# Two batches' factor products in a row, with smaller edits around them, in a two-layer LoRA kernel

## The chip, the cores and the metric

The kernel runs on one core of one Trainium2 chip. The metric is the device time of one execution in microseconds (us); three runs of the kernel before gave 287.18, 287.47 and 287.54.

## The reference

Two residual layers follow each other, each a linear layer with a bias and with a low-rank adapter that each of the 8 batches picks by an index (x is 8 x 256 x 1024, rank 16, 32 adapters each, all float32):

```python
def layer0(x, idx, W, b, As, Bs):
    h = einsum('bti,bir->btr', x, As[idx])
    return einsum('bti,oi->bto', x, W) + b + 2 * einsum('btr,bro->bto', h, Bs[idx])
def layer1(x, idx, W, b, A, B):
    h = einsum('bsd,brd->bsr', x, A[idx])
    return einsum('bsd,od->bso', x, W) + b + einsum('bsr,bor->bso', h, B[idx])
x = x + layer0(x, itok_B_0_23, ...)
x = x + layer1(x, itok_B_6_15, ...)
```

## The kernel before

**The algebra.** The kernel multiplies the two weight matrices once, (I + W0^T)(I + W1^T), and then applies the one product to all batches. Both levels use a Strassen-like scheme on 2 x 2 quadrants of 512 x 512: seven products M1 to M7 for the weights, and for each batch seven products p1 to p7 of 128 x 512 by 512 x 512, from four quadrants A11, A21, A12, A22 of x, four sums S1 to S4 of them, and seven right sides (B11, B21, B22, T1 to T4). Each float32 operand is split into a high part (a cast to fp32r, on ScalarE, ACT in the profile) and a low part (a subtraction, on VectorE, DVE), and a product takes three fp32r passes: high by high, high by low, low by high. A product p is so twelve matmuls of 512 columns (`product`, L1194).

**What is added by small products.** The adapters and biases come in through a stack of 98 rows per batch. The kernel builds, ahead of the batches, `g` (`gt_passes`, `turn`, `g_copy`), the rows `r` (`r_passes`, with `s_t` times `b1_raw` in plain float32 at L1155 and L1160) and the bias rows `c` (`ones_b` times `bias_sum`, L1173, in plain float32, one bank for each half). The rows r, the rows b1 and the rows c, each as high and low parts, go out to `rb_rows` in DRAM (`bounce`, L319, and L327) and come back for each batch (`load_rb`). For each batch, `h_product` (L1217) multiplies x by the batch's two factor matrices: 8 matmuls of 256 columns in plain float32, whose left sides have 32 columns each, on four column tiles of the array. For batch 0 the sum runs over the high and the low parts of x, so there are 16. `stack_h` on DVE adds the four partial results and splits them; `ranks` (L1207) puts stack times rows on top of a bank.

**Order.** Each engine has one hand-written order. TensorE (PE): M1, M2, g's first half, M7, `turn(0)`, M3, s_t's product, r's passes, M6, c, g's second half, M5, M4 (with `turn(1)` inside), then the batches. Batch 0 goes p1, p6, h(0), p7, p2, p5, p4, `fill_z` (a rank product that waits for u4), h(1), p3; a later batch b goes p1, p6, p2, p5, p7, h(b+1), p4, fill_z, p3. In M1 the last step over k goes through all four banks with the high pass and then through all four with the low ones; M2 adds onto these banks once ACT has copied each one out (`m1_kept`). There is one buffer `xr` for the raw x of a batch (in the place of v22), and x of batch b+1 is loaded quadrant by quadrant over x of batch b as its users finish (`load_x`, L263). SyncE (SP) issues nearly all DMAs in one order.

Of the kernel before, what the change touches and what calls it, by code (L numbers as in the profile page):

```python
# [39 lines left out]
def lora_pair(nc, xT, U11, V11, W0, W1T, A0, B0T, A1T, B1, b0, b1, idx0, idx1, out):  # L40
# [22 lines left out]
    with ExitStack() as ctx:  # L63
# [11 lines left out]
        raw_a = sb("raw_a", [P, 4, QUAD], F32)  # L75
# [11 lines left out]
        aa = sb("aa", [P, 2 * HALF], F32)[:, 0:HALF].rearrange("p (s k c) -> p s k c", s=2, k=KT)  # L87
# [5 lines left out]
        s_t = sb("s_t", [P, BR], F32)  # L93
# [17 lines left out]
        b1_hl = b0w_flat[:, 0:2 * D].rearrange("p (s n) -> p s n", s=2)  # L111
# [4 lines left out]
        c_hl = [c_rows[32 * part:32 * part + B, :] for part in range(2)]  # L116
# [25 lines left out]
        xr = raw("v22").rearrange("p (j n) -> p j n", j=4)  # L142

        x_first = [late[:, part, :].rearrange("p (j n) -> p j n", j=4) for part in range(2)]
# [5 lines left out]
        stage_q = raw_a[:, 0:3, :].rearrange("p s (k n) -> p (s k) n", n=HALF)  # L150
# [4 lines left out]
        u4 = [stage_q[:, 2, :], stage_q[:, 8, :]]  # L155
        c21, c22, c12 = u2, u3, u4

        def s_raw(j, b):

            if b == 0 and j in (S3, S4):  # L160
                return xr[:, A21 if j == S3 else A12, :]
            return {S1: rows[:, 0, :], S2: rows[:, 1, :], S3: stage_q[:, 9, :], S4: stage_q[:, 10, :]}[j]

        def x_raw(j, b):
            return xr[:, j, :] if j <= A22 else s_raw(j, b)
# [15 lines left out]
        x_landed = [sem(f"x_landed{j}") for j in range(4)]  # L181
        a0_landed = [sem(f"a0_landed{s}") for s in range(2)]
        r_bounced = sem("r_bounced")
        bounced = sem("bounced")
# [40 lines left out]
        st_step = sem("st_step")  # L225
        r_summed = sem("r_summed")
# [3 lines left out]
        b1_hi_made = sem("b1_hi_made")  # L230
        b1_lo_made = sem("b1_lo_made")
        c_hi_made = sem("c_hi_made")
        c_lo_made = sem("c_lo_made")
# [29 lines left out]
        def _(sp):  # L263
            def load_x(b):
                for j in (A11, A21, A12, A22):
                    if b >= 1:

                        if j != A21 or b == 1:
                            sp.wait_ge(op_lo[j], b)
                        for s in {A11: (S2, S3), A21: (S1, S3), A12: (S4,), A22: (S1,)}[j]:  # L270
                            sp.wait_ge(s_made[s], b)
                        if j in (A21, A12) and b == 1:
                            sp.wait_ge(op_lo[S3 if j == A21 else S4], b)
                    if b >= 2:
                        sp.wait_ge(h_summed, b)
                    sp.dma_start(xr[:, j, :], xT[b, :, j, :]).then_inc(x_landed[j], DMA)
# [9 lines left out]
            def store(b, q, h, name, tile):  # L286
                sp.wait_ge(made[name], b + 1)
                sp.dma_start(out[b * T + q * P:b * T + (q + 1) * P, h * HALF:(h + 1) * HALF], tile[b % 2]
                             ).then_inc(stored[name], DMA)
# [19 lines left out]


# [5 lines left out]
            def bounce(n, src, done):  # L316
                for g, part in enumerate((0, 1, 0)):
                    at = (2 * g + n) * RK
                    sp.dma_start(rb_dram[:, at:at + RK, :], words(src[:, part, :])).then_inc(done, DMA)  # L319
# [5 lines left out]
            sp.wait_ge(c_lo_made, NH)  # L325
            for part in range(2):
                sp.dma_start(rb_dram[:, 6 * RK + part, :], words(c_hl[part])).then_inc(bounced, DMA)  # L327
            sp.wait_ge(r_bounced, 3 * DMA)
            sp.wait_ge(bounced, 5 * DMA)
# [27 lines left out]
        def _(pool):  # L357
# [39 lines left out]
            for b in range(B):  # L397
                i1 = adapter(B + b)
                pool.dma_start(b1_raw[b * RK:(b + 1) * RK, :],
                               B1[bass.ds(i1, 1), :, :].rearrange("s r n -> (s r) n")).then_inc(b1_landed, DMA)  # L400
            for b in range(2, B):
                load_a0(b)

        @block.scalar
        def _(act):
# [48 lines left out]
            def high_x(j, b):  # L454
                if j <= A22:
                    act.wait_ge(x_landed[j], (b + 1) * DMA)
                else:
                    act.wait_ge(s_made[j], b + 1)
                if b >= 1:

                    act.wait_ge(p_done[LAST_USE[j]], b)
                    if j <= A22 and b == 1:
                        act.wait_ge(h_summed, b)
# [66 lines left out]
            act.wait_ge(r_summed, 1)  # L530
# [7 lines left out]
            act.wait_ge(summed["us1"], 1)  # L538
            high("us1")
# [4 lines left out]
            high("vt1")  # L544
            high("vt4")
            act.wait_ge(b1_landed, B * DMA)
            for h in range(NH):
                nc.scalar.copy(b1_hl[:, 0, h * HALF:(h + 1) * HALF], b1_raw[:, h * HALF:(h + 1) * HALF]
                               ).then_inc(b1_hi_made, 1)
# [3 lines left out]
            for h in range(NH):  # L553
                act.wait_ge(c_summed, h + 1)
                nc.scalar.copy(c_hl[0][:, h * HALF:(h + 1) * HALF], b_banks[1 + h][0:B, :]).then_inc(c_hi_made, 1)
            for m in (1, 2):
                act.wait_ge(c_lo_made, m)
                put_e(m)
# [6 lines left out]
            for j in (A11, A21, A12, A22):  # L565
                high_x(j, 0)
# [51 lines left out]
        def _(dve):  # L618
# [104 lines left out]

            def sum_s1(b):
                dve.wait_ge(x_landed[A21], (b + 1) * DMA)
                dve.wait_ge(x_landed[A22], (b + 1) * DMA)
                if b >= 1:
                    dve.wait_ge(op_lo[S1], b)
                nc.vector.tensor_tensor(s_raw(S1, b), xr[:, A21, :], xr[:, A22, :], ALU.add).then_inc(s_made[S1], 1)

            def sum_s2(b):
                dve.wait_ge(x_landed[A11], (b + 1) * DMA)
# [3 lines left out]
                nc.vector.tensor_tensor(s_raw(S2, b), s_raw(S1, b), xr[:, A11, :], ALU.subtract).then_inc(s_made[S2], 1)  # L736

            def sum_s3(b):
                if b == 0:

                    dve.wait_ge(op_lo[A21], 1)
                else:
                    dve.wait_ge(x_landed[A11], (b + 1) * DMA)
                    dve.wait_ge(x_landed[A21], (b + 1) * DMA)
                    if b == 1:

                        dve.wait_ge(lo[SLOT["t1"]], filled("t1", 1))
                    dve.wait_ge(op_lo[S3], b)
                nc.vector.tensor_tensor(s_raw(S3, b), xr[:, A11, :], xr[:, A21, :], ALU.subtract).then_inc(s_made[S3], 1)

            def sum_s4(b):
                if b == 0:
                    dve.wait_ge(op_lo[A12], 1)
                else:
                    dve.wait_ge(x_landed[A12], (b + 1) * DMA)
                    if b == 1:
                        dve.wait_ge(lo[SLOT["t1"]], filled("t1", 1))
                    dve.wait_ge(op_lo[S4], b)
# [637 lines left out]
```

## Time and profile before

| | |
|---|---|
| median of 3 runs | 287.47 us |
| the profiled execution | 287.28 us |
| its span in the profile | 285.7 us |
| PE busy | 280.7 us (98%) |
| PE weight loads busy | 223.7 us (78%) |
| DVE busy | 215.3 us (75%) |
| ACT busy | 102.9 us (36%) |
| POOL busy | 18.7 us (7%) |
| granted TensorE clock | 1.00 over nearly the whole span |

Busy time of PE is modelled: a matmul of 512 columns is shown as 0.39 us long, and the next one starts while it is still shown as running. What a matmul costs in a stream is the distance between the starts of two.

### The profile page before, as it was taken

How to read it: one execution, taken by the hardware profiler on the slowest of the kernel's cores; microseconds unless marked ns; L12 is line 12 of the kernel's file. 1: busy time of each engine (PE TensorE's matmuls, PEld its weight loads, DVE VectorE, ACT ScalarE, POOL GpSimd, SP SyncE). 2: the span in 40 equal slices, each digit the busy share in tenths (PEclk: the TensorE clock that was granted, in tenths of full speed). 3: DMA queues.
4: the chain of work that ended last, by engine and by line, in shares of the span. 5: the costliest groups of instructions: out<-in, count | busy, mean ns of one | idle time of the engine just before them, and what ended most of it. 6: DMA issues, size and time to landing. Idle time of an engine off the chain costs nothing.

```text
span 285.7 us, 3887 instructions
## 1 busy us (share of the span) xinstructions
PE 280.7 (98%) x1333; PEld 223.7 (78%) x1333; DVE 215.3 (75%) x322; ACT 102.9 (36%) x143; POOL 18.7 (7%) x43
## 2 busy tenths in 40 slices
PE   7999999999999999999999999999999999999996
PEld 5878888877878888787878878878878878878885
DVE  4789999999889999688775684784784684774413
ACT  3675464333696654323131141141141131141100
POOL 3333201300000001000000000000000000000000
PEclk9999999999999999999999999999999999999999
DMA  6997000200445360002811712711701711711013
GB/s 204 409 411 292 28 1 11 56 9 0 154 141 209 147 210 17 2 37 76 242 45 76 246 40 77 245 41 73 252 37 73 241 39 73 240 39 73 37 39 111
DMA packets 15370, 33.95 MB, mean 119 GB/s; under 512 B 2390, under 2 KB 2646, under 8 KB 15351
## 3 DMA queue, kind: packets, MB, share of 16 engines
q1 hardware_dynamic: 14178, 31.60, 31.7%
q0 software_dynamic: 1024, 2.10, 2.3%
q8 instruction: 11, 0.18, 0.3%
q14 instruction: 9, 0.07, 0.1%
q10 hardware_dynamic: 148, 0.00, 0.0%
HBM read 22.09 MB, written 11.60 MB: 118 GB/s over the span
## 4 chain that ended last, share of the span: by engine, by line
PE 93%; DMA 4%; SPq 1%; ACT 1%; issue 0%; DVE 0%
PE bank L1201 18%; PE bank L1202 18%; PE bank L1203 18%; PE bank L1049 8%; PE bank L1054 8%; PE bank L1053 8%; DMA raw_a<-W1T 4%; PE bank L1233 3%; PE bank L1208 3%; PE bank L1081 1%; PE bank L1083 1%; PE bank L1082 1%; PE bank L1067 1%; PE bank L1069 1%; PE bank L1068 1%; SPq L293 1%
## 5 line engine op out<-in xcount | busy, mean ns | idle before, releaser
L1201 PE MATMUL bank<-ops,late 128*128 128x512 f32 x192 | 75.8, 395 | 0.0
L1202 PE MATMUL bank<-ops,late 128*128 128x512 f32 x192 | 75.0, 391 | 0.0
L1203 PE MATMUL bank<-ops,late 128*128 128x512 f32 x192 | 74.8, 389 | 0.0
L464 ACT CAST late<-raw_a 128x512 fp32r<-128x512 f32 x41 | 25.2, 622 | 65.7 <-PE bank L1208 38.0
L1201 PEld LDWEIGHTS bank<-ops,late 128*128 128x128 f32 x192 | 36.1, 188 | 10.4 <-issue 2.9
L1054 PE MATMUL bank<-ops 128*128 128x512 f32 x112 | 43.6, 390 | 0.0
L1053 PE MATMUL bank<-ops 128*128 128x512 f32 x112 | 43.6, 389 | 0.0
L1203 PEld LDWEIGHTS bank<-ops,late 128*128 128x128 f32 x192 | 36.1, 188 | 7.8
L1202 PEld LDWEIGHTS bank<-ops,late 128*128 128x128 f32 x192 | 36.1, 188 | 7.4
L1049 PE MATMUL bank<-ops 128*128 128x512 f32 x112 | 40.2, 397 | 0.5 <-ACT raw_b L492 0.5
L722 DVE TENSOR_TENSOR late<-raw_a,late 128x512 fp32r<-128x512 f32 x41 | 27.7, 688 | 2.6 <-ACT late L464 2.4
L1049 PEld LDWEIGHTS bank<-ops 128*128 128x128 f32 x112 | 20.6, 188 | 6.3 <-issue 1.1
L1053 PEld LDWEIGHTS bank<-ops 128*128 128x128 f32 x112 | 21.0, 188 | 4.5 <-issue 0.2
L1054 PEld LDWEIGHTS bank<-ops 128*128 128x128 f32 x112 | 21.0, 188 | 4.4
L648 DVE TENSOR_TENSOR ops<-raw_a,ops 128x2048 fp32r<-128x2048 f32 x9 | 20.6, 2286 | 0.0
L464 ACT CAST late<-rows 128x512 fp32r<-128x512 f32 x16 | 9.7, 621 | 29.8 <-DVE rows L736 29.0
L831 DVE TENSOR_TENSOR raw_a<-bank,raw_a 128x512 f32<-128x512 f32 x8 | 5.5, 692 | 18.7 <-PE bank L1208 18.6
L416 ACT CAST ops<-raw_a 128x2048 fp32r<-128x2048 f32 x9 | 17.1, 1914 | 6.8 <-DVE raw_a L651 3.7
L648 DVE TENSOR_TENSOR ops<-raw_b,ops 128x2048 fp32r<-128x2048 f32 x6 | 13.6, 2287 | 1.9 <-ACT ops L416 1.9
L416 ACT CAST ops<-raw_b 128x2048 fp32r<-128x2048 f32 x6 | 11.5, 1915 | 10.0 <-PE bank L1155 5.0
L722 DVE TENSOR_TENSOR late<-rows,late 128x512 fp32r<-128x512 f32 x16 | 10.9, 688 | 4.8 <-ACT late L464 4.8
L390 POOL DMA_DIRECT2D a_raw<-A x8 | 4.3, 543 | 145.5 <-DVE aa L772 144.1
(149 smaller groups left out, 373.0 us busy)
## 6 DMA issues: line engine op xcount, KB each, us to landing
raw_a<-xT SPq DMA_DIRECT2D x32, 256.0 KB, 4.2
out<-raw_a SPq DMA_DIRECT2D x27, 256.0 KB, 2.0
a<-rb_rows SPq DMA_DIRECT2D x8, 392.0 KB
raw_a<-W1T SPq DMA_DIRECT2D x2, 1024.0 KB, 12.5
raw_b<-W SPq DMA_DIRECT2D x2, 1024.0 KB, 16.2
rb_rows<-late SPq DMA_DIRECT2D x3, 512.0 KB
rb_rows<-b0w SPq DMA_DIRECT2D x3, 512.0 KB
raw_a<-U SPq DMA_DIRECT2D x4, 256.0 KB, 4.8
```

Source lines behind the costliest of these rows:

```text
L416: nc.scalar.copy(op(q, 0), raw(q)).then_inc(hi[SLOT[q]], 1)
L464: nc.scalar.copy(x_op(j, 0), x_raw(j, b)).then_inc(op_hi[j], 1)
L648: nc.vector.tensor_tensor(op(q, 1), raw(q), op(q, 0), ALU.subtract).then_inc(lo[SLOT[q]], 1)
L722: nc.vector.tensor_tensor(x_op(j, 1), x_raw(j, b), x_op(j, 0), ALU.subtract).then_inc(op_lo[j], 1)
L1049: return mm(bank[:, :], left(u, 0, k, m), op_k(v, 0, k), start=(k == 0 and not on_top), stop=False, skip_group_check=on_top)
L1053: mm(bank[:, :], left(u, 0, k, m), op_k(v, 1, k), start=False, stop=False, skip_group_check=on_top)
L1054: return mm(bank[:, :], left(u, 1, k, m), op_k(v, 0, k), start=False, stop=(k == KH - 1), skip_group_check=on_top)
L1201: mm(bank[:, :], hi, t_op(t, 0, k), start=(start and k == 0), stop=False, skip_group_check=not start)
L1202: mm(bank[:, :], hi, t_op(t, 1, k), start=False, stop=False, skip_group_check=not start)
L1203: last = mm(bank[:, :], lo, t_op(t, 0, k), start=False, stop=(k == KH - 1), skip_group_check=not start)
L1208: return mm(bank[:, :], h_stack[b % 2][0:STACK, q * P:(q + 1) * P], rb[b % 2][:, h * HALF:(h + 1) * HALF], start=False, stop=True, skip_gr ...
L1233: last = mm(banks[6 + s][j * CT:(j + 1) * CT, 0:T], aa[:, s, k, :], part[:, 2 * kh:2 * kh + 2, tok], start=(k < TILES and n == 0), stop=(k ...
```

## The change

1. **x in two buffers.** `xr` becomes a list of two: v22's place for even batches and t1's place for odd ones. A batch's x comes in two DMAs of two quadrants each in place of four; `load_x(b+2)` is issued at the start of batch b, and `load_x(1)` after the low part of t1 is made.
2. **Factor products in pairs.** h(0) is computed ahead of p1(0), with 8 matmuls from the raw x; then, in each even batch b, h(b+1) and h(b+2) follow each other behind p7(b). Batch 0 takes the order of the others. DVE makes the factor operands of both batches in a row (`factors`).
3. **Raw sums.** S1 and S4 share a place, S3 moves to spare room beside `aa`, A21's high and low parts are no longer made for batch 0, and a few DVE steps change places.
4. **Single passes for cores times rows.** s_t and b1 are split into high and low parts; s_t times b1 becomes three fp32r passes for each half, behind all of r's passes. The b1 rows are split earlier and bounced to DRAM ahead of `load_x(0)`.
5. **Bias in column tiles.** The two halves of `bias_sum` are summed by 32-column left sides on two column tiles of one bank, and split by one cast and one subtraction.
6. **First product bank by bank.** In M1's last step over k each bank gets its high pass and then its two low ones; ACT casts v21's first half behind its first copy out of M1's banks.
7. The ones rows of the stack are set on POOL early, in place of DVE late; each store waits for the store before it of the same name.

```diff
+        xr = [raw(q).rearrange("p (j n) -> p j n", j=4) for q in ("v22", "t1")]
...
+        s_raw = {S1: rows[:, 0, :], S2: rows[:, 1, :], S3: aa_room[:, HALF:2 * HALF], S4: rows[:, 0, :]}
...
             def load_x(b):
+                if b == 1:
+                    sp.wait_ge(lo[SLOT["t1"]], filled("t1", 1))
+                if b >= 2:
+                    for j in (A11, A12, A22):
+                        sp.wait_ge(op_lo[j], b - 1)
+                    for s in (S1, S2, S3, S4):
+                        sp.wait_ge(s_made[s], b - 1)
+                    sp.wait_ge(h_summed, b - 1)
+                for h in range(NH):
+                    sp.dma_start(xr[b % 2][:, 2 * h:2 * h + 2, :], xT[b, :, 2 * h:2 * h + 2, :]
+                                 ).then_inc(x_landed[b % 2][h], DMA)
...
+            sp.wait_ge(b1_split, 2)
+            bounce(1, b1_hl, b1_bounced)
...
-            sp.wait_ge(b1_lo_made, NH)
-            bounce(1, b1_hl, bounced)
...
-                if b + 1 < B:
-                    load_x(b + 1)
+                if b + 2 < B:
+                    load_x(b + 2)
+                if b == 0:
+                    load_x(1)
...
-            high_half("v21", 0)
             for m in range(KH):
+                if m == 1:
+                    high_half("v21", 0)
                 act.wait_ge(m_done[1], m + 1)
...
+            act.wait_ge(lo[SLOT["us4"]], filled("us4", 1))
+            act.wait_ge(b1_landed, B * DMA)
+            nc.scalar.copy(b1_hl[:, 0, :], b1_raw).then_inc(b1_split, 1)
+            act.wait_ge(st_step, 2)
+            nc.scalar.copy(s_hl[:, 0, :], s_t).then_inc(st_step, 1)
...
             low("vt2")
+            dve.wait_ge(st_step, 3)
+            nc.vector.tensor_tensor(s_hl[:, 1, :], s_t, s_hl[:, 0, :], ALU.subtract).then_inc(st_step, 1)
+            dve.wait_ge(b1_split, 1)
+            nc.vector.tensor_tensor(b1_hl[:, 1, :], b1_raw, b1_hl[:, 0, :], ALU.subtract).then_inc(b1_split, 1)
...
-            dve.wait_ge(lo[SLOT["us4"]], filled("us4", 1))
+            dve.wait_ge(r_summed, NH)
+            dve.wait_ge(b1_bounced, 3 * DMA)
             combine("t2", "d11", "t3", ALU.add)
...
-            dve.wait_ge(bounced, 5 * DMA)
-            for s in range(2):
-                nc.vector.memset(h_stack[s][6 * RK:6 * RK + 2, :].bitcast(F32), 1.0).then_inc(ones_set, 1)
...
+                if k < KH - 1:
+                    for m in range(KH):
+                        high_pass("u11", "v11", a_banks[m], m, k)
...
                 for m in range(KH):
+                    if k == KH - 1:
+                        high_pass("u11", "v11", a_banks[m], m, k)
                     last = low_passes("u11", "v11", a_banks[m], m, k)
...
-            mm(a_banks[0][:, :], s_t[:, :], b1_raw[:, 0:HALF], start=False, stop=True).then_inc(r_summed, 1)
...
-            mm(a_banks[1][:, :], s_t[:, :], b1_raw[:, HALF:D], start=False, stop=True).then_inc(r_summed, 1)
+            for h in range(NH):
+                cols = slice(h * HALF, (h + 1) * HALF)
+                mm(a_banks[h][:, :], s_hl[:, 0, :], b1_hl[:, 0, cols], start=False, stop=False)
+                mm(a_banks[h][:, :], s_hl[:, 0, :], b1_hl[:, 1, cols], start=False, stop=False)
+                mm(a_banks[h][:, :], s_hl[:, 1, :], b1_hl[:, 0, cols], start=False, stop=True).then_inc(r_summed, 1)
...
-            for h in range(NH):
-                cols = slice(h * HALF, (h + 1) * HALF)
-                mm(b_banks[1 + h][:, :], ones_b[:, :], bias_sum[:, cols], start=True, stop=True).then_inc(c_summed, 1)
+            for j in range(NH):
+                last = mm(b_banks[2][j * CT:(j + 1) * CT, :], ones_b[:, 0:CT], bias_sum[:, j * CW:(j + 1) * CW],
+                          start=True, stop=True)
+            last.then_inc(c_summed, 1)
...
-            p1(0)
-            p6(0)
             h_product(0)
-            p7(0)
-            p2(0)
-            p5(0)
-            p4(0)
-            fill_z(0)
-            h_product(1)
-            p3(0)
-            for b in range(1, B):
+            for b in range(B):
                 p1(b)
                 p6(b)
                 p2(b)
                 p5(b)
                 p7(b)
-                if b + 1 < B:
-                    h_product(b + 1)
+                if b % 2 == 0:
+                    for n in (b + 1, b + 2):
+                        if n < B:
+                            h_product(n)
                 p4(b)
                 fill_z(b)
```

## Rows read from the trace of the kernel before

**Rows 1.** The page, busy time and share of the span of each engine.

```profile
PE 280.7 (98%) x1333; PEld 223.7 (78%) x1333; DVE 215.3 (75%) x322; ACT 102.9 (36%) x143; POOL 18.7 (7%) x43
```

**Rows 2.** Busy time in two stretches: PE, PEld, DVE, ACT, POOL, then PEclk, DMA share, GB/s.

```profile
78.00:98.00 20.00, 20.00 (x86) 15.88 (x85) 18.42 (x17) 15.63 (x21) 0.00 (x0) 1.00 0.46 161
200.00:240.00 40.00, 40.00 (x198) 31.59 (x197) 26.82 (x51) 9.98 (x17) 0.54 (x1) 1.00 0.35 117
```

**Rows 3.** Timeline of PE, end of M1 and start of M2: start, duration, idle before.

```profile
16.30 0.39 PE L1054 MATMUL bank<-ops 128*128 128x512 f32 x1
17.17 2.10 PE L1049 MATMUL bank<-ops 128*128 128x512 f32 x8 [0.48 <-ACT raw_b L492]
```

**Rows 4.** Timeline of ACT, v21's first half and the four copies out of M1.

```profile
15.49 1.05 ACT L413 CAST ops<-raw_a 128x1024 fp32r<-128x1024 f32 x1 [0.84 <-DMA raw_a<-W1T]
16.45 2.04 ACT L492 COPY raw_b<-bank 128x512 f32<-128x512 f32 x4
```

**Rows 5.** Timeline of DVE: M1's last low part, us3, and v22's low part.

```profile
12.52 0.68 DVE L638 TENSOR_TENSOR ops<-raw_b,ops 128x512 fp32r<-128x512 f32 x1
...
18.36 2.29 DVE L651 TENSOR_TENSOR raw_a<-raw_b,raw_a 128x2048 f32<-128x2048 f32 x1 [0.56 <-DMA raw_b<-W]
...
42.32 2.28 DVE L648 TENSOR_TENSOR ops<-raw_a,ops 128x2048 fp32r<-128x2048 f32 x1
```

**Rows 6.** Timeline of PE, the first turn and the start of M3.

```profile
44.51 0.60 PE L1075 MATMUL bank<-ident,g_all 128*128 128x128 f32 x4
44.86 0.48 PE L1049 MATMUL bank<-ops 128*128 128x512 f32 x1
```

**Rows 7.** Timeline of PE around s_t times b1's first half.

```profile
63.14 0.39 PE L1083 MATMUL bank<-ops,b0w 128*128 128x512 f32 x1
...
64.46 0.39 PE L1082 MATMUL bank<-ops,b0w 128*128 128x512 f32 x1
```

**Rows 8.** Timeline of PE around the bias product.

```profile
81.33 0.39 PE L1054 MATMUL bank<-ops 128*128 128x512 f32 x1
...
83.50 0.39 PE L1068 MATMUL bank<-ops,a 128*128 128x512 f32 x1
```

**Rows 9.** Timeline of PE around h(0), in batch 0.

```profile
116.22 0.39 PE L1203 MATMUL bank<-ops,late 128*128 128x512 f32 x1
...
118.74 0.40 PE L1202 MATMUL bank<-ops,late 128*128 128x512 f32 x1
```

**Rows 10.** Timeline of PE around h(2), in batch 1.

```profile
148.23 0.39 PE L1203 MATMUL bank<-ops,late 128*128 128x512 f32 x1
148.55 1.07 PE L1233 MATMUL bank<-raw_a,aa 128*32 128x256 f32 x16
...
149.89 0.40 PE L1202 MATMUL bank<-ops,late 128*128 128x512 f32 x1
```

**Rows 11.** Timeline of PE, batch 0's two rank products ahead of h(1).

```profile
129.67 0.90 PE L1208 MATMUL bank<-a,b0w 98*128 98x512 f32 x2
130.50 1.07 PE L1233 MATMUL bank<-raw_a,aa 128*32 128x256 f32 x16
```

**Rows 12.** Timeline of PE, the first matmul of p1(0).

```profile
111.01 0.39 PE L1201 MATMUL bank<-ops,late 128*128 128x512 f32 x1
```

**Rows 13.** Timeline of DVE: vt1's low part, the end of factors(0), t1's low part, stack_h(0)'s last step.

```profile
79.41 2.29 DVE L648 TENSOR_TENSOR ops<-raw_b,ops 128x2048 fp32r<-128x2048 f32 x1 [1.91 <-ACT ops L416]
...
110.38 0.22 DVE L772 COPY aa<-g_all 128x128 f32<-128x128 f32 x1
...
117.25 2.28 DVE L648 TENSOR_TENSOR ops<-raw_a,ops 128x2048 fp32r<-128x2048 f32 x1
...
122.06 0.42 DVE L800 TENSOR_TENSOR b0w<-h_sum,b0w 32x256 fp32r<-32x256 f32 x1
```

**Rows 14.** Timeline of SP, the issue of t_cols.

```profile
69.66 0.34 SPq L307 DMA_DIRECT2D t_cols<-t_sums  x1
```

**Rows 15.** The page, the issues of x's DMAs: count, KB each, us to landing.

```profile
raw_a<-xT SPq DMA_DIRECT2D x32, 256.0 KB, 4.2
```

More of the change, by code:

```diff
@@ L74, in lora_pair @@
         ops = sb("ops", [P, 6, 2, QUAD], F32R)
-        raw_a = sb("raw_a", [P, 4, QUAD], F32)
+        with nc.sbuf_tensor("raw_a", [P, 4, QUAD], F32) as raw_a:
+            pass
+        b1_hl = sb("b1_hl", [P, 2, D], F32R)
+        sb("raw_a_rest", [P, 3, QUAD], F32)
         with nc.sbuf_tensor("raw_b", [P, 6, QUAD], F32) as raw_b:
@@ L115, in lora_pair @@
         a_diff_raw, b_sum_raw = factor_sums[:, 0, :], factor_sums[:, 1, :]
-        c_hl = [c_rows[32 * part:32 * part + B, :] for part in range(2)]
+        CW = HALF
+        c_hl = [c_rows[0:NH * CT, part * CW:(part + 1) * CW] for part in range(2)]
         gt_raw = g_all[:, KH:KT, :].rearrange("p k n -> p (k n)")
@@ L308, in _, with bounce @@
                          allow_slow_non_contiguous=True).then_inc(t_landed, DMA)
+            def bounce(n, src, done):
+                for g, part in enumerate((0, 1, 0)):
+                    at = (2 * g + n) * RK
+                    sp.dma_start(rb_dram[:, at:at + RK, :], words(src[:, part, :])).then_inc(done, DMA)
+            sp.wait_ge(b1_split, 2)
+            bounce(1, b1_hl, b1_bounced)
             sp.wait_ge(lo[SLOT["v22"]], filled("v22", 1))
@@ L544, in _ @@
             high("vt1")
+            act.wait_ge(summed["us1"], 1)
+            high("us1")
             high("vt4")
[L546 to L549 removed]
             put_e(3)
@@ L552, in _ @@
             high("d11")
[L553 to L558, printed above, removed]
+            put_e(1)
+            act.wait_ge(c_summed, 1)
+            nc.scalar.copy(c_hl[0], b_banks[2][0:NH * CT, :]).then_inc(c_split, 1)
+            act.wait_ge(c_split, 2)
+            put_e(2)
             gt_copy(1)
@@ L961, in _ @@
             low("t3")
-            for j in (A11, A21, A12, A22):
+            for j in (A11, A12, A22):
                 low_x(j, 0)
@@ L990, in _ @@
             low_d21(3)
+            stack_h(0)
+            factors(2)
+            low("t1")
             make_u2(0)
-            low("t1")
-            stack_h(0)
             low("t4")
-            make_u3(0)
             for j in (A11, A12):
                 low_x(j, 1)
+            make_u4(0)
             sum_s1(1)
@@ L1082, in r_passes @@
                     mm(bank[:, :], high_b, op_k(q, 1, k), start=False, stop=False)
-                    mm(bank[:, :], low_b, op_k(q, 0, k), start=False, stop=False)
+                    last = mm(bank[:, :], low_b, op_k(q, 0, k), start=False, stop=False)
+                return last
             pe.wait_ge(warm_set, 1)
@@ L1221, in h_product @@
                 pe.wait_ge(aa_ready, 2 * (b + 1))
-                for j in (A11, A21, A12, A22):
-                    if b == 0:
-                        pe.wait_ge(op_lo[j], 1)
-                    else:
-                        pe.wait_ge(x_landed[j], (b + 1) * DMA)
+                for h in range(NH):
+                    pe.wait_ge(x_landed[s][h], (b // 2 + 1) * DMA)
+                if b == 0:
+                    pe.wait_ge(lo[SLOT["d22"]], filled("d22", KH))
+                    pe.wait_ge(summed["t1"], KH)
                 if b >= 2:
                     pe.wait_ge(h_added, b - 1)
-                parts = [words(part) for part in x_first] if b == 0 else [xr]
-                for n, part in enumerate(parts):
-                    for k in range(KT):
-                        kh, tok, j = k // KH, slice(k % KH * P, (k % KH + 1) * P), k % TILES
-                        last = mm(banks[6 + s][j * CT:(j + 1) * CT, 0:T], aa[:, s, k, :],
-                                  part[:, 2 * kh:2 * kh + 2, tok], start=(k < TILES and n == 0),
-                                  stop=(k >= KT - TILES and n == len(parts) - 1))
+                for k in range(KT):
+                    kh, tok, j = k // KH, slice(k % KH * P, (k % KH + 1) * P), k % TILES
+                    last = mm(banks[6 + s][j * CT:(j + 1) * CT, 0:T], aa[:, s, k, :],
+                              xr[s][:, 2 * kh:2 * kh + 2, tok], start=(k < TILES), stop=(k >= KT - TILES))
                 last.then_inc(h_summed, 1)
```

147 lines of the change are left out of this document (60 added, 87 removed).

## The prediction

> **What bounds the kernel now.** I read the page's busy times first: PE is busy for 280.7 of 285.7 us [rows 1], and in a 40 us stretch of the steady batches for 40.00 of 40.00 us at a granted clock of 1.00 (the 2.4 GHz level), with DVE at 26.82 and ACT at 9.98 [rows 2]. Then I read PE's timeline by the distance between starts. The matmuls of 512 columns follow each other at 0.227 us. So what the change takes out of PE's stream is worth its full distance, and work on other engines costs nothing while it stays ahead of PE. The only wait of PE behind ACT that the view of waits shows inside the stream is the 0.48 us at the start of M2 [rows 3].
>
> **The factor products.** Between the last pass ahead of h(2) and the second pass behind it lie 149.89 - 148.23 = 1.66 us, where two ordinary distances are 0.45: a site of 8 matmuls (16 instructions) costs 1.21 us. At h(0), with 16 matmuls (32 instructions), 118.74 - 116.22 - 0.45 = 2.07 us [rows 9, 10]. The difference, 0.86, is the price of 8 matmuls in the stream; the other 0.35 of a site is paid once, for going over to the column tiles and back. Before, there are eight sites: 2.07 + 7 x 1.21 = 10.54 us. After, h(0) and h(7) stand alone and three pairs stand together: 2 x 1.21 + 3 x (2 x 0.86 + 0.35) = 8.63 us. Gain **1.91 us** (0.86 from batch 0's half, 1.05 from three sites). The second product of a pair writes another bank (6, then 7), which no row shows; h(0)'s second round of eight over the same bank is the nearest, so I take 0.35 once. If each product of a pair pays it, the gain is 0.86. Behind a site some ten matmuls come at 0.23 to 0.24 in place of 0.227, up to 0.1 a site; that is an upper bound of 0.3 more, not in the sum.
>
> **s_t times b1.** 64.46 - 63.14 = 1.32 us less 0.45 is 0.87 for one plain float32 matmul [rows 7], so two cost 1.73. They become six fp32r passes at 0.227, 1.36. Gain **0.37 us**. The new operands are off the path: b1's low part is one DVE step of some 1.2 us and s_t's of 0.3 behind vt2's low part, so both are there by about 66.2, and PE wants them behind all r passes, at about 68.8.
>
> **The bias.** 83.50 - 81.33 - 0.45 = 1.72 us now [rows 8]. With 32-column left sides on two tiles of one bank the work halves if the two run side by side, as the four tiles do in an h site: 16 instructions of 256 columns in 0.86 us, where the plain matmul above gives 3.4. That is 0.86, and a site's 0.35 comes on top: 1.21. Gain **0.51 us**. If the two tiles run one behind the other it is a loss of 0.35: both ends stay in the range. I take the first since the h sites are the same form. Here the Trainium skill speaks against the edit (TensorEngine Tiling (Array Packing), Key Properties): changing the tiling mode drains the engine, and this edit adds a mode change in a place that had none. The trace agrees that a change costs something, 0.35 us a site [rows 9, 10]; without that drain the gain here would be 0.86, and with it 0.51.
>
> **M1 bank by bank.** Now PE starts M2 at 17.17 although M1's last pass started at 16.30, because ACT casts v21's half (landed late, 15.49 to 16.54) and only then copies M1's bank 0 (16.45 to 17.04) [rows 3, 4]. After, bank 0 is finished three passes into the last step, near 14.7, and is copied before v21 lands; M2 can start at the end of that cast, near 16.65, and its next banks arrive with the copies at 0.5 us each, about as PE asks for them. M2 starts 0.5 us earlier. The last step's high passes now wait for the low parts too, which is free: they are done at 13.20 [rows 5], and PE comes to the step at 16.30 - 11 x 0.227 = 13.80. But what is late next? M3 needs v22's low part, which DVE ends at 42.32 + 2.28 = 44.60 [rows 5]. DVE runs nearly without a gap from us3 on, which waits for a DMA (18.36), so this end does not move. PE starts M3 at 44.86 [rows 6] and would come 0.5 earlier; it will stand until about 44.73. So only **0.13 us** of the 0.5 is kept. (Bounds 0 and 0.5.)
>
> **Batch 0's wait.** Two rank products of 0.227 from 129.67 end at 130.12, and a site starts 0.09 later, near 130.22, but h(1) starts at 130.50 [rows 11]: fill_z waits for u4. In the new order p7, two h and p4 stand between p5 and fill_z. Gain **0.28 us**.
>
> **The work that must stay hidden.** (a) h(0) now stands ahead of p1(0), 111.01 now [rows 12], and 1.0 us earlier with the terms so far (0.13 + 0.37 + 0.51): 110.0. It needs factors(0), which DVE ends at 110.60 [rows 13]. On DVE fall away one low part of x (0.6), two memsets (0.6) and half of c's subtraction (0.6), 0.2 is added for s_t; b1's step only moves. So 109.0, or near 107.1 if the 1.91 us of idle at 79.41 [rows 13] is filled by the steps that moved ahead. One us of cover or more. (b) t1's low part comes behind stack_h(0) (from the end of t1's low part at 119.53 to 122.48, 2.9 us [rows 13]) and factors(2): from M4's last block, 110.0 + ACT's cast = 110.9, + 1.2 + 2.9 + 0.3 + 2.3 = 117.6, or 118.4 from DVE's own chain. p5(0) asks for it at 110.0 + 1.2 + three products of 2.72 + 0.2 = 119.6. Cover 1.2 to 2. (c) x(1) is issued when t1's low part is done and lands within about 5 us (4.2 for one of four DMAs now [rows 15]), near 123; h(1) asks at 119.6 + 5.4 = 125.0. (d) POOL's and SP's moved steps: the two memsets on POOL stand ahead of the loads of A0 for batches 2 and up, which wait for factors(0) anyway; the stores' extra waits are for DMAs two us long, a batch old. (e) SP: the b1 rows (three DMAs of 512 KB, 1.57 MB) go out behind t_cols, from 70.0 [rows 14], then x(0) (1.05 MB), then r (1.57 MB). The r, b1 and c rows now take the stretch from 78 to 98 at 161 GB/s [rows 2]. At that rate b1 alone is out by 79.8, by 86.3 if x(0) shares the queues evenly; DVE's step for t2 waits for it, and comes to it at about 84. In the steady batches x(b+2) is issued a whole batch ahead, and DVE has 13 of 40 us free [rows 2]; the double factors add 0.3 us to one batch in two. All of (a) to (e) at nothing.
>
> **Sum.** 1.91 + 0.37 + 0.51 + 0.13 + 0.28 = 3.20 us. The profiled execution took 287.28, 1.58 more than its span; so 284.08. The median of the runs is 0.19 higher. I take 284.2.
>
> **The rivals.**
>
> 1. The forecast, 283.4 to 284.7. Chance 0.62.
> 2. A cover of batch 0 is too short: DVE's chain or x(1) comes late, and PE stands for 0.8 to 2.5 us ahead of h(0), p5 or h(1). For: DVE is busy for 18.42 of 20 us there [rows 2], and (b) has only 1.2 us by one count. Against: every move but one takes work off DVE. 285.0 to 286.7, say 285.6. Chance 0.15.
> 3. The bias tiles run one behind the other: 0.86 less gain, 285.1. For: no row shows two tiles. Against: the h sites. Chance 0.08.
> 4. Pairs pay 0.35 twice: 1.05 less gain, 285.2. Chance 0.07. That pairing does nothing at all is this case.
> 5. Slower than before: the bounces. b1, x(0) and r are 4.2 MB from 70.0; at 161 GB/s they end near 96, while DVE's first low part of x, which waits for ACT's cast and that for r's bounce, is due near 93. Three us late less 1.1 of cover costs 1.9, and leaves 286.1. It decides from an end at about 98.0 on (150 GB/s), where the 3.2 are used up with 0.6 more; at 145 GB/s the time is 289. For: the same rows ran at 161 only. Against: x alone is no such slow traffic, its four DMAs land in 4.2 us [rows 15]. Chance 0.05.
> 6. Nothing to tell: 287 to 288, some smaller losses together. Chance 0.03.
>
> **How the numbers follow.** About 0.2% (0.57 us) is what a measurement of this kernel tells from no change. Cases 1 to 4 are all faster by more: 0.92. Case 6 and the part of 5 between give 0.04 for the same, the rest of 5 gives 0.04 for slower. The lower end of the range is the forecast with all upper bounds (0.37 more at M2, 0.3 behind the sites, 0.35 if the bias tiles' mode change is free): 283.1. The upper end takes in cases 3 and 4 and most of 2: 286.0.
>
> **What would show it.** Right: PE's idle ahead of M2 gone and a new one of some 0.3 us ahead of M3; one site of 32 instructions and about 2.07 us in batches 0, 2, 4; the bias site at about 1.2 us; no row of PE waiting in batch 0; a period of two batches shorter by 0.35. Wrong: a wait of PE for DVE at h(0), p5(0) or h(1), a wait of DVE ahead of t2's sum for a DMA, or a bias site near 2.1 us.

## The result, and the profile after

The changed kernel's median is 284.72 us (283.67 to 285.29, 6 runs), beside 287.50 for the kernel before (286.85 to 287.71, 6 runs): a ratio of 0.990, 95% interval 0.988 to 0.993, or 2.8 us less. It was run twice more, beside the kernel before each time (287.40 and 287.48): 284.29 us (284.20 to 284.69, 5 runs; 0.990, 0.988 to 0.992) and 284.78 us (283.93 to 285.27, 6 runs; 0.990, 0.988 to 0.992). Over all 17 runs the median is 284.62. The forecast was 284.2 in a range of 283.1 to 286.0. The profiled execution took 284.42 us, 2.86 less than that of before, with a span of 282.8.

The page of the changed kernel, busy times and the issues of x (before: [rows 1, 15]):

```profile
PE 278.3 (98%) x1319; PEld 224.5 (79%) x1319; DVE 215.2 (76%) x318; ACT 102.3 (36%) x141; POOL 19.3 (7%) x45
...
raw_a<-xT SPq DMA_DIRECT2D x16, 512.0 KB, 4.8
```

PE is 2.4 us less busy; the other engines' busy times moved by 0.8 us or less. The windows of [rows 2], with the first 3 us of M1 ahead of them (columns as there):

```profile
5.00:8.00 3.00, 2.97 (x8) 2.01 (x7) 2.60 (x6) 1.60 (x3) 1.21 (x2) 1.00 0.95 351
78.00:98.00 20.00, 20.00 (x89) 15.62 (x88) 17.84 (x15) 11.25 (x16) 0.00 (x0) 1.00 0.52 188
200.00:240.00 40.00, 40.00 (x200) 32.11 (x199) 26.75 (x48) 9.72 (x17) 0.53 (x1) 1.00 0.34 116
```

PE's timeline, at the places that the prediction named (before: [rows 3, 6, 8, 9, 10]):

```profile
5.50 2.05 PE L1065 MATMUL bank<-ops 128*128 128x512 f32 x4
7.35 0.59 PE L1069 MATMUL bank<-ops 128*128 128x512 f32 x1
7.78 0.40 PE L1070 MATMUL bank<-ops 128*128 128x512 f32 x1
...
17.35 0.39 PE L1070 MATMUL bank<-ops 128*128 128x512 f32 x1
17.58 2.00 PE L1065 MATMUL bank<-ops 128*128 128x512 f32 x8
...
44.84 0.60 PE L1091 MATMUL bank<-ident,g_all 128*128 128x128 f32 x4
45.19 0.48 PE L1065 MATMUL bank<-ops 128*128 128x512 f32 x1
...
81.33 0.39 PE L1070 MATMUL bank<-ops 128*128 128x512 f32 x1
81.64 1.05 PE L1197 MATMUL bank<-rows,ones_b 128*32 128x512 f32 x4
82.96 0.39 PE L1084 MATMUL bank<-ops,a 128*128 128x512 f32 x1
...
110.23 0.39 PE L1070 MATMUL bank<-ops 128*128 128x512 f32 x1
110.55 1.07 PE L1258 MATMUL bank<-raw_a,aa 128*32 128x256 f32 x16
...
111.89 0.40 PE L1228 MATMUL bank<-ops,late 128*128 128x512 f32 x1
...
125.35 0.39 PE L1229 MATMUL bank<-ops,late 128*128 128x512 f32 x1
125.67 1.93 PE L1258 MATMUL bank<-raw_a,aa 128*32 128x256 f32 x32
127.87 0.40 PE L1228 MATMUL bank<-ops,late 128*128 128x512 f32 x1
...
279.70 0.28 PE L1292 MATMUL bank<-a,b0w 98*128 98x256 f32 x1
```

The row of 32 instructions is a pair: two sites in one, 127.87 - 125.35 - 0.45 = 2.07 us, where two sites apart cost 2.42. Count from the start of M3 to the start of the last matmul: 45.19 to 279.70 is 234.51 us, beside 237.73 before (44.86 to 282.59). So 3.22 us went out of that stretch. But M3 starts 0.33 us later than in [rows 6], though M2 follows M1 without the wait of [rows 3]. The first rows say where that comes from: four passes of M1 take 7.35 - 5.50 = 1.85 us, where the kernel before took 1.02, and the next distance is 0.43, twice the usual 0.227. I read that as the 1.2 GHz level: the same 0.43 stand beside a granted clock of 0.51 in the kernel with the late bias sums, below. It is a reading of distances, for the clock column shows 1.00 here.

What the covers of batch 0 became can be read on ACT and on DVE (before, for DVE: [rows 13]):

```profile
94.53 1.67 ACT L484 CAST late<-raw_a 128x512 fp32r<-128x512 f32 x3 [3.03 <-DMA rb_rows<-late]
```

```profile
95.19 1.90 DVE L745 TENSOR_TENSOR late<-raw_a,late 128x512 fp32r<-128x512 f32 x3 [1.36 <-ACT late L484]
...
109.88 0.22 DVE L790 COPY aa<-g_all 128x128 f32<-128x128 f32 x1
...
117.22 2.28 DVE L671 TENSOR_TENSOR ops<-raw_a,ops 128x2048 fp32r<-128x2048 f32 x1
```

ACT stands 3.03 us for r's bounce to DRAM (rival 5's first half), and DVE 1.36 behind ACT's first cast. factors(0) ends at 110.10, 0.45 us ahead of h(0); the prediction gave this cover (a) 1.0 us or more. t1's low part ends at 119.50 and p5(0) starts at 120.12: cover (b) is 0.6, not 1.2 to 2. Both held in this profile, so the forecast's time held.

### The profile page after: what moved, and what is told of

It is laid out like the page before. It is cut to its first block, busy times and chain, and to the rows that moved or that the text cites. A ratio compares the mean times of both kernels' runs of the same rounds, so it can differ in the third digit from the quotient of the medians.

```text
span 282.8 us, 3853 instructions
## 1 busy us (share of the span) xinstructions
PE 278.3 (98%) x1319; PEld 224.5 (79%) x1319; DVE 215.2 (76%) x318; ACT 102.3 (36%) x141; POOL 19.3 (7%) x45
## 4 chain that ended last, share of the span: by engine, by line
PE 98%; DVE 0%; issue 0%
PE bank L1227 18%; PE bank L1228 18%; PE bank L1229 18%; PE bank L1065 9%; PE bank L1069 9%; PE bank L1070 9%; PE bank L1258 3%; PE bank L1234 3%; PE bank L1083 1%; PE bank L1105 1%; PE bank L1097 1%; PE bank L1099 1%; PE bank L1098 1%; PE bank L1085 1%; PE bank L1084 1%; PE bank L1167 1%
## 5 line engine op out<-in xcount | busy, mean ns | idle before, releaser
L484 ACT CAST late<-rows 128x512 fp32r<-128x512 f32 x24 | 14.7, 622 | 52.3 <-DVE rows L762 26.0
L484 ACT CAST late<-raw_a 128x512 fp32r<-128x512 f32 x24 | 14.8, 624 | 30.6 <-PE bank L1234 21.1
L1065 PEld LDWEIGHTS bank<-ops 128*128 128x128 f32 x112 | 21.4, 192 | 5.1 <-ACT ops L431 0.7
L1070 PEld LDWEIGHTS bank<-ops 128*128 128x128 f32 x112 | 21.2, 189 | 4.5
L1069 PEld LDWEIGHTS bank<-ops 128*128 128x128 f32 x112 | 21.2, 189 | 4.5
L745 DVE TENSOR_TENSOR late<-rows,late 128x512 fp32r<-128x512 f32 x24 | 16.6, 691 | 5.0 <-ACT late L484 4.8
L745 DVE TENSOR_TENSOR late<-raw_a,late 128x512 fp32r<-128x512 f32 x24 | 16.3, 687 | 3.8 <-ACT late L484 3.7
```

The costliest lines, as they stand in the source:

```text
L484: nc.scalar.copy(x_op(j, 0), x_raw(j, b)).then_inc(op_hi[j], 1)
L745: nc.vector.tensor_tensor(x_op(j, 1), x_raw(j, b), x_op(j, 0), ALU.subtract).then_inc(op_lo[j], 1)
L1065: return mm(bank[:, :], left(u, 0, k, m), op_k(v, 0, k), start=(k == 0 and not on_top), stop=False, skip_group_check=on_top)
L1069: mm(bank[:, :], left(u, 0, k, m), op_k(v, 1, k), start=False, stop=False, skip_group_check=on_top)
L1070: return mm(bank[:, :], left(u, 1, k, m), op_k(v, 0, k), start=False, stop=(k == KH - 1), skip_group_check=on_top)
```

## The experiments

Four questions were left: does the fee of 0.35 us a site explain the pairs; is the M1 edit worth 0.13; how near was batch 0 to a wait, and what made it so; and do two column tiles run side by side. Where not said otherwise, an experiment is one edit of the changed kernel. "M3 to end" is the stretch defined above: 234.51 in the changed kernel, free of what happens at the start.

| kernel | median us (range, runs) | ratio to before, 95% | M3 to end, us |
|---|---|---|---|
| changed, first | 284.72 (283.67–285.29, 6) | 0.988–0.993 | 234.51 |
| sites apart | 285.12 (284.36–285.33, 4) | 0.989–0.995 | 235.56 |
| M1 edit undone | 284.67 (284.42–284.96, 4) | 0.988–0.993 | 234.50 |
| SP reordered | 283.92 (283.22–284.32, 4) | 0.985–0.991 | 234.48 |
| DVE delayed | 285.22 (283.48–286.40, 7) | 0.989–0.995 | 235.40 |
| changed, second | 284.29 (284.20–284.69, 5) | 0.988–0.992 | 234.69 |
| bias sums late | 287.03 (285.81–289.68, 12) | 0.997–1.003 | 239.33 |
| bias late and SP | 284.40 (283.93–285.53, 6) | 0.988–0.992 | 234.66 |
| SP and DVE delayed | 284.74 (283.83–285.40, 4) | 0.987–0.993 | 234.49 |
| changed, third | 284.78 (283.93–285.27, 6) | 0.988–0.992 | 234.50 |
| SP, again | 284.35 (283.75–284.48, 4) | 0.987–0.991 | 234.49 |
| SP and half the bias | 284.14 (283.61–284.85, 4) | 0.986–0.990 | 234.51 |
| bias product twice | 284.24 (1 run) | | 234.48 |

### The sites of a pair taken apart

```diff
-                    for n in (b + 1, b + 2):
-                        if n < B:
-                            h_product(n)
+                    h_product(b + 1)
                 p4(b)
                 fill_z(b)
+                if b % 2 == 0 and b + 2 < B:
+                    h_product(b + 2)
```

> The changed kernel with the second factor product of each pair moved behind p4 and fill_z: the same work on every engine, three more changes to the column tiles and back. Theory (a site has a fixed fee of 0.35 us, and the matmuls behind it come up to 0.1 us late in sum): two batches take 42.66 us from site to site in place of 42.21, and the span grows by 1.0 to 1.35 us. Rival (the gain came from the second buffer of x or from other waits, not from fewer sites): the span stays within 0.3 us of the changed kernel's.

PE's timeline of this kernel, in batch 2:

```profile
168.00 1.07 PE L1258 MATMUL bank<-raw_a,aa 128*32 128x256 f32 x16
...
172.45 1.07 PE L1258 MATMUL bank<-raw_a,aa 128*32 128x256 f32 x16
```

Same matmuls, same operands, no wait, only apart: M3 to end is 235.56, longer by 1.05 us, three times 0.35. Two batches take 42.56 us (168.00 to 210.56), and 42.21 in pairs (125.67 to 167.88). Rival 4 falls. Two things stay open. The kernel before takes 42.66 (148.55 to 191.21), and the 0.10 between did not come back with the sites, against the expectation. And the median rose by only 0.4 to 0.5 us, in ranges that overlap: the price rests on the rows and not on the medians.

### M1's edit undone

```diff
+                for m in range(KH):
+                    high_pass("u11", "v11", a_banks[m], m, k)
                 for m in range(KH):
-                    if k == KH - 1:
-                        high_pass("u11", "v11", a_banks[m], m, k)
                     last = low_passes("u11", "v11", a_banks[m], m, k)
...
+            high_half("v21", 0)
             for m in range(KH):
-                if m == 1:
-                    high_half("v21", 0)
```

> The changed kernel with M1 in its old order, and v21's first half cast ahead of all copies out of M1. My account of this edit: it takes away PE's wait ahead of M2 only where TensorE reaches the 2.4 GHz level early enough, and then DVE's end of v22's low part (near 44.7) holds M3. So undone, M3 starts at 44.86 with an early clock (0.13 us later than it would) and at 45.19, as in the changed kernel, with a late one: the time moves by 0.0 to 0.15 us. Rival (the 0.5 us ahead of M2 comes through in full): 0.5 us slower.

PE waited 0.49 us ahead of M2 again, as in [rows 3], and M3 started at 45.12. The median, 284.67, is that of the changed kernel. What holds M3 shows when its start is measured from the start of us3 on DVE (before: 18.36 to 44.86, 26.50 us, [rows 5, 6]). With M1's edit undone it is 18.66 to 45.12, 26.46. In the seven profiles of kernels with the edit, and with DVE's order as it was, in which M3 waited beyond its turn it is 26.33 or 26.34: for instance 18.46 to 44.79 in the second run of the changed kernel. So the edit gives 0.13 to 0.17, about as forecast, where PE comes to M3 in time (the medians cannot tell that from nothing), and nothing where the first four passes of M1 take as long as in the first and the third profile of the changed kernel (1.85 and 1.84 us): PE then comes late by itself. PE's timeline in that second run of the changed kernel, whose start was fast:

```profile
5.52 1.17 PE L1065 MATMUL bank<-ops 128*128 128x512 f32 x4 [0.28 <-ACT ops L431]
6.53 0.39 PE L1069 MATMUL bank<-ops 128*128 128x512 f32 x1
...
44.08 0.60 PE L1091 MATMUL bank<-ident,g_all 128*128 128x128 f32 x4
44.79 0.47 PE L1065 MATMUL bank<-ops 128*128 128x512 f32 x1
```

Four passes take 1.01 us; the turn starts at 44.08, and M3 follows 0.71 later, where it is 0.35 without a wait (44.84 to 45.19 above). Here is the new idle ahead of M3, 0.36 us long, that the prediction asked for.

### SP's queue: t_cols behind r's bounce

SP issues a load of t's sums (t_cols) that waits for their own way to DRAM (t_sums). In both kernels it stands ahead of b1's bounce, which in the changed kernel has x(0) and r's bounce behind it. The edit moves it:

```diff
-            sp.wait_ge(t_zeroed, 1)
-            sp.wait_ge(t_bounced, DMA)
-            sp.dma_start(t_cols[RK:2 * RK, :], ...).then_inc(t_landed, DMA)
...
             bounce(0, r_hl, r_bounced)
+            sp.wait_ge(t_zeroed, 1)
+            sp.wait_ge(t_bounced, DMA)
+            sp.dma_start(t_cols[RK:2 * RK, :], ...).then_inc(t_landed, DMA)
```

> The changed kernel with SP's load of t_cols (which waits 7 us for t_sums to land) moved behind the bounce of r, so that the b1 rows start near 66.3 in place of 70.25. ACT waits 3.0 us for r's bounce in the changed kernel, DVE 1.4 us behind it, and factors(0) ends only 0.45 us before h(0). Theory (the cover is thin but holds): ACT's wait for r's bounce falls to near 0, factors(0) ends about 1.4 us earlier, and the time stays the same within 0.3 us. Rival (in some executions PE stands in batch 0): 0.3 to 0.8 us faster, and a narrower spread of times.

It was run once more, beside another set of the changed kernel:

> The changed kernel with t_cols behind the bounce of r, once more with more rounds. Theory (DVE's cover ahead of h(0) is so short in the changed kernel that some executions lose 0.1 to 0.3 us there, and the edit gives 1.4 us of cover): 0.1 to 0.3 us faster than the control, no wait of PE in batch 0. Rival (the 283.92 of the first try was the luck of the start): the same as the control within 0.1 us.

SP's timeline of the changed kernel, and then of this one:

```profile
62.47 0.36 SPq L313 DMA_DIRECT2D t_sums<-t_sum  x1
69.88 0.33 SPq L316 DMA_DIRECT2D t_cols<-t_sums  x1
70.25 4.16 SPq L322 DMA_DIRECT2D rb_rows<-b_hl  x3
74.53 3.60 SPq L282 DMA_DIRECT2D raw_a<-xT  x2
78.17 4.01 SPq L322 DMA_DIRECT2D rb_rows<-late  x3
```

```profile
62.10 0.36 SPq L313 DMA_DIRECT2D t_sums<-t_sum  x1
65.90 4.10 SPq L317 DMA_DIRECT2D rb_rows<-b_hl  x3
70.13 2.80 SPq L282 DMA_DIRECT2D raw_a<-xT  x2
72.97 3.38 SPq L317 DMA_DIRECT2D rb_rows<-late  x3
76.45 0.51 SPq L332 DMA_DIRECT2D t_cols<-t_sums  x1
```

SP's waits in the changed kernel, line, us in total, times, longest:

```profile
SPq L315 <- DMA t_sums<-t_sum: 7.0, 1, 7.0
```

The queue stood for 7 us behind the landing of one tiny transfer. Without that, r's bounce goes out 5.2 us earlier, and no wait for it is left on ACT (this kernel's ACT, then its DVE):

```profile
90.70 1.66 ACT L483 CAST late<-raw_a 128x512 fp32r<-128x512 f32 x3
```

```profile
107.74 0.22 DVE L789 COPY aa<-g_all 128x128 f32<-128x128 f32 x1
```

factors(0) ends at 107.96 and h(0) starts at 109.86: the cover is 1.90 us, where it was 0.45. M3 to end is 234.48, as before the edit, for PE never waited there in the first place. The medians, 283.92 and in a second set of runs 284.35, lie 0.7 and 0.3 us below the 284.62 over the 17 runs of the changed kernel; all eight runs lie between 283.22 and 284.48, with a median of 284.2. The intervals overlap, so a gain of some 0.4 us is likely and not shown.

### DVE delayed by 1.4 us, with and without SP's edit

Two steps of 128 x 512 whose result is written again right behind them stand ahead of t2's low part:

```diff
+            for n in range(PAD):
+                ...
+                nc.vector.tensor_tensor(op_k("t2", 1, 0), raw_k("t2", 0), op_k("t2", 0, 0), ALU.subtract
+                                        ).then_inc(padded, 1)
             low("t2")
```

> The changed kernel with two useless DVE steps (128 x 512, about 0.6 us each, the same low part written twice more) ahead of t2's low part in batch 0. Theory (DVE's cover ahead of h(0) is 0.45 us): PE stands for 0.7 to 1.0 us ahead of h(0) with DVE as the releaser, and the time grows by as much. Rival (DVE's chain has the 1 to 2 us of cover that I counted): no wait of PE over 0.3 us, the same time.

> The two useless DVE steps again, now with t_cols behind the bounce of r. Theory (the late bounce of r eats DVE's cover, 1.4 us of it): the 0.92 us that PE stood ahead of h(0) fall to 0.1 us or nothing, and the time is that of the changed kernel. Rival (the cover is set by something else on DVE): PE stands for 0.6 us or more again.

PE's timeline with the delay alone:

```profile
111.33 1.07 PE L1267 MATMUL bank<-raw_a,aa 128*32 128x256 f32 x16 [0.92 <-DVE aa L792]
```

1.44 us more on DVE become 0.92 of waiting ahead of h(0), and M3 to end is longer by 0.89: the cover of the changed kernel was about 0.5 us, as its trace says. With SP's edit beside it there is no wait (factors(0) ends at 110.04, h(0) starts at 110.48), and the median is 284.74. So SP's queue was what made this cover thin. The second profile of the changed kernel shows how thin, with a wait of PE for DVE at h(0), which the prediction had named as a sign of being wrong:

```profile
110.36 1.07 PE L1258 MATMUL bank<-raw_a,aa 128*32 128x256 f32 x16 [0.17 <-DVE aa L790]
```

There M3 had started 0.40 us earlier than in the first, and h(0) caught up with DVE; its M3 to end is the 234.50 of the others and these 0.17.

### DVE's bias sums moved behind v22's low part

If DVE's v22 is what M3 waits for, work ahead of it on DVE that nobody needs yet should go behind it.

```diff
-            bias_first(0)
-            bias_first(1)
             dve.wait_ge(m1_kept, KH)
             low("us4")
             make_e1(0)
             low("v22")
             make_e1(1)
+            bias_first(0)
+            bias_first(1)
```

> The changed kernel with DVE's first four bias sums (2.7 us) moved behind v22's low part and the second of e1's sums. Theory (DVE's chain to v22's low part, not PE, sets M3's start): that low part ends one to two us earlier, near 42.9 to 43.8 because ACT's cast of us4 then holds DVE, M3 follows its own turn at 0.35 us without a further gap, and M3 starts 0 to 0.5 us earlier, most where M2 starts early: 0.1 to 0.4 us faster. Rival (the sums moved back delay vt2's low part and M6): a wait of PE for DVE near 70, 0 to 2 us slower.

The timeline of DVE in this kernel, then of ACT, then of PE:

```profile
39.08 2.29 DVE L671 TENSOR_TENSOR ops<-raw_a,ops 128x2048 fp32r<-128x2048 f32 x1 [2.00 <-ACT ops L438]
...
41.88 2.28 DVE L671 TENSOR_TENSOR ops<-raw_a,ops 128x2048 fp32r<-128x2048 f32 x1
...
44.69 2.73 DVE L709 SCALAR_TENSOR_TENSOR rows<-raw_b,b_raw,rows 128x512 f32<-128x512 f32 x4
```

```profile
97.44 1.67 ACT L484 CAST late<-raw_a 128x512 fp32r<-128x512 f32 x3 [4.60 <-DMA rb_rows<-late]
```

```profile
113.07 1.07 PE L1258 MATMUL bank<-raw_a,aa 128*32 128x256 f32 x16 [2.99 <-DVE aa L790]
114.07 0.80 PE L1227 MATMUL bank<-ops,late 128*128 128x512 f32 x1
114.66 0.63 PE L1228 MATMUL bank<-ops,late 128*128 128x512 f32 x1
115.09 0.63 PE L1229 MATMUL bank<-ops,late 128*128 128x512 f32 x1
...
117.58 0.40 PE L1229 MATMUL bank<-ops,late 128*128 128x512 f32 x1
```

The theory held for M3, which starts at 44.46, 0.35 behind its turn, and failed for the time. The bias sums were not ahead of v22 for nothing: they filled a wait for ACT's cast of us4. Taken away, they leave 2.00 us of idle; v22's low part ends at 44.16 in place of 44.80, and the 2.7 us of sums now come on top of DVE's chain. They reach factors(0) through SP's queue: t_sum is made 2.0 us later on DVE, r's bounce goes out at 80.16 in place of 78.17, and ACT stands for it for 4.60 us, DVE for 2.93 behind ACT. h(0) waits 2.99 us, and that costs more than itself, for the matmuls behind it come at 0.43 (from 114.66 to 117.22, six of them): eight distances from 114.07 take 3.51 us, 1.98 in the changed kernel (111.55 to 113.53). A window of this kernel over that stretch, columns as in [rows 2]:

```profile
114.10:117.60 3.50, 3.50 (x13) 2.82 (x10) 3.44 (x9) 0.00 (x0) 0.71 (x2) 0.51 0.58 188
```

The granted clock is 0.51 behind the wait, the 1.2 GHz level: 1.53 us lost there beside the 2.99 of the wait, of 4.82 in all that M3 to end is longer (0.2 of the rest is lost at the bias product). The median, 287.03, lies level with the kernel before (0.997 to 1.003), but the 12 runs are of two kinds. Six have a mean granted clock of 0.998 to 1.000 over the whole kernel and took 285.81 to 286.67 us; six, the profiled one among them, have 0.988 to 0.994 and took 287.40 to 289.68. So the low clock comes in about half of the executions. How long PE waits in the others no trace shows.

> Both schedule edits at once: the bias sums late, and t_cols behind the bounce of r. Expected: factors(0) ends 1.5 to 2 us ahead of h(0), no wait of PE behind M2, M3 at the end of its turn, 0.1 to 0.5 us faster than the changed kernel and no slower than either edit alone. Rival: none of it reaches the end, the same time within 0.2 us.

With SP's edit beside it the wait is gone, and ACT waits for no bounce; the median is 284.40. The loss was h(0)'s wait, and SP's edit is enough to cancel it. But factors(0) ends at 110.76 and h(0) starts at 110.84: a cover of 0.08 us where 1.5 to 2 were expected, and no gain over the changed kernel beside it (284.29).

> t_cols behind the bounce of r, and only two of DVE's four first bias sums moved behind v22's low part. DVE waited 2.0 us for ACT's cast of us4 when all four were moved; with two kept it should wait about 0.7, so v22's low part ends 0.5 us earlier and DVE's chain behind it comes 0.8 us later, which the cover from the SP edit (1.9 us) holds. Theory: M3 starts with its turn in all executions, 0.1 to 0.4 us faster than with the SP edit alone. Rival: DVE's later chain makes PE stand ahead of h(0) or p5, no gain or a loss.

With SP's edit and only `bias_first(1)` moved, DVE waits 0.65 us for us4's cast and ends v22's low part at 44.00; M3 then followed its turn without a wait in the profile (44.88 behind 44.52). That decides nothing, for M1's first four passes took 1.84 us in it, and after such a start M3 follows its turn in the changed kernel too. The median is 284.14, ratio 0.986 to 0.990. Its interval overlaps with those of SP's edit alone and of the changed kernel: at best a few tenths of a microsecond.

### The bias product doubled

```diff
-            for j in range(NH):
-                last = mm(b_banks[2][j * CT:(j + 1) * CT, :], ...)
+            for i in range(2 * NH):
+                j = i % NH
+                last = mm(b_banks[2][i * CT:(i + 1) * CT, :], ...)
```

> The changed kernel with the bias product doubled: the same two halves once more on the other two column tiles of the same bank (nothing reads them). Theory (column tiles run side by side): from the last pass of M6 to the second of g's passes 1.63 us as in the changed kernel, within 0.1. Rival (they run one behind the other in part): 0.4 to 0.9 us more.

PE's timeline of it:

```profile
81.13 0.39 PE L1070 MATMUL bank<-ops 128*128 128x512 f32 x1
81.45 1.07 PE L1198 MATMUL bank<-rows,ones_b 128*32 128x512 f32 x8
82.78 0.39 PE L1084 MATMUL bank<-ops,a 128*128 128x512 f32 x1
```

Twice the instructions, on four tiles in place of two, take 1.65 us from pass to pass, beside 1.63 (81.33 to 82.96). The tiles run side by side: one behind the other, the second two would have added about 0.87 us or more, by the price of a plain matmul in [rows 7]. Rival 3 falls.

### The changed kernel again

The second set of runs of the changed kernel stood beside the kernels with late bias sums and the one with SP's edit and the delay, the third beside the last three.

> The changed kernel once more, unchanged, for its spread and for a second trace of its start. Theory (the work behind M3 is fixed, the start varies from execution to execution with the landing of the first loads and with when TensorE leaves the 1.2 GHz level): from M3's first matmul to the last matmul 234.5 us as in the first trace, where the kernel before has 237.73; M3 starts anywhere from 44.5 to 45.2; the median lies between 284.0 and 284.8. Rival (the shortfall of 0.5 us against my forecast is a loss somewhere in the batches): M3 to end longer than 234.7 in this trace.

> The changed kernel as control, beside two versions with other schedules on the same chip. Expected: a median of 284.2 to 284.8 us, and in the trace either no wait of PE in batch 0 or one of at most 0.3 us ahead of h(0).

## Why the prediction was right

**The sum, term by term.** The sites: 1.91 forecast. h(0) now costs 1.21 us and a pair 2.07, exactly the prices taken from [rows 9, 10]. From M4's last pass to the end the kernel is 2.34 us shorter, 0.15 more than the 1.91 and batch 0's 0.28 together; that lies within the 0.3 named as upper bound for the slower matmuls behind a site. That they are the reason is not shown: the three sites taken apart brought back 1.05 us and nothing on top. (The 3.4 us that the prediction's working has for a plain matmul's rate is 3.5, 8 times half of 0.87; nothing hangs on it.) The bias: 2.17 became 1.63, so 0.54 (0.51 forecast). s_t times b1: 0.33 (0.37 forecast), read from M3's start to the start of M6's last pass, 36.14 us beside 36.47; the six passes came at 0.233, not at 0.227, and that is the difference. Batch 0's wait for u4 is gone. These make 3.21 of the 3.22 us that went out behind M3's start; 3.07 was forecast.

**The bias's mode change.** The first experiment shows that going to the column tiles and back costs 0.35 us, and the site of the bias is as long as with such a fee: 1.18 us for a work put at 0.86. By the Trainium skill (TensorEngine Tiling (Array Packing), Key Properties) a change of mode drains the engine; these traces agree that it costs time, 0.35 us for the way there and back, and do not show what the time goes into.

**M1.** The reason held: PE's wait ahead of M2 went (a fast start leaves some 0.2 us of it: in the second profile M2 starts at 16.72 behind a pass at 16.28), DVE's v22 low part took its place, and 0.13 to 0.17 of the 0.5 us stayed. But it stays only in executions whose first matmuls are fast.

**What the forecast left out.** The profiled pair gives 2.86 = 3.22 from M3 on, less 0.33 from M3's later start, less 0.03 around. The forecast priced the start by one execution, as if it were fixed. The time of M1's first four passes was 1.02 us in the kernel before and 1.85 in the changed one; over the 14 profiles of all kernels here it was between 0.99 and 1.13 in eight and between 1.39 and 1.85 in six, with no rule by kernel to be seen. The changed kernel itself had 1.85, 1.01 and 1.84. Since only one trace of the kernel before was taken, how often its own start is late is open, and so is whether this explains why the medians differ by 2.8 and not by 3.2.

**The covers.** This is the step that was mis-sized. The prediction gave (a) 1.0 us "or more" and (b) 1.2 to 2; they were 0.45 and 0.6 in the first profile, and (a) was 0.17 too short in the second and 1.32 in the third (factors(0) done at 109.28, h(0) at 110.60), where ACT's wait for the bounce was 2.16 and M3 started late. The reason is rival 5's: the bounces ended near 94.4, where the rival had 96, and ACT stood for 3.03 us. The prediction had priced these 3 us less 1.1 of cover at 1.9 and gave it a small chance; in fact DVE lost only 1.36 of ACT's 3.03, and factors(0) ended at 110.10, still 0.50 earlier than in [rows 13], but not at the 109.0 that the prediction had. That this error cost nothing is in part luck: the cover left was 0.45 us in one profile, and in the next PE stood for 0.17. That t_cols waits for 7 us at the head of SP's queue was in [rows 14] by its issue time alone; the prediction took 70.0 as given and did not ask what it waited for.

## What to carry to other kernels

Two sites that pay a fixed fee for a change of tiling mode are worth putting together, and the fee can be read beforehand from two places with different amounts of the same work. After a gain on the bottleneck, measure each cover again in the new trace: a cover that went from over 1 us to 0.45 costs nothing until the next small edit, and then a wait of 3 us can bring the low clock with it, as it did in six of twelve runs here. When a transfer on a critical queue is late, look at the wait at the head of the queue before looking at bandwidth.

## What the runs showed of the hardware that was not expected

- The start of TensorE's 2.4 GHz level differs between executions: four passes at the start of M1 took from 0.99 to 1.85 us, the same kernel included (1.85, 1.01, 1.84). The Trainium skill (TensorE: Matmul & The Clock Gate, What you observe) says that the point of transition varies by half a microsecond either way from run to run. These traces agree that it varies, and show more: the distance is still 0.43 at 7.35 us in the first profile of the changed kernel, and 0.25 on average from 5.52 on in the second. The clock column showed 1.00 in the window from 5 to 8 us all the same, so the level there has to be read from distances (0.43 against 0.227 us).
- After 2.99 us without a matmul, PE started at the high level and fell to 0.51 about a microsecond later, for 3.4 us (from near 114.1 to 117.5 in the kernel with the late bias sums; the h site at 113.07 still takes its usual 1.00 us). The mean clocks of that kernel's runs say that it happened in six of twelve. A wait of 0.92 us in the one profile that has it brought no such fall.
- Column tiles with plain float32 ran side by side whether two or four were used: 1.63 and 1.65 us from pass to pass for one and for two times the work.
- A load that waited for a transfer of 512 bytes to DRAM, 4 from each partition, stood for 7 us at the head of its queue (62.47 to 69.88), longer than the 4.8 us that 512 KB of x took to land.
